# A two-layer graph network on one core: ten slots for streamed weights instead of six, and each weight piece in three or five transfers instead of two

## The reference

```python
h = relu(layernorm(x))
q, k, v = h @ wq.T + bq, h @ wk.T + bk, h @ wv.T + bv
q2, k2, v2 = q @ wiq.T + biq, k @ wik.T + bik, v @ wiv.T + biv     # 16 heads of 64
attn = softmax(q2 k2^T / 8 + mask(edges, edge_type_5))
x = x + (attn v2) @ wo.T + bo
h = relu(layernorm(x))
u = h @ root + bias
for r in range(8):
    u = u + mean_over_edges_of_type_r(h) @ weight[r]
z = concat([u, h]) @ w_gate + b_gate
x = x + tanh(u) * z + h * (1 - z)
```

## Time and profile before

| | us |
|---|---|
| median of 3 runs | 229.99 (228.32 to 234.5) |
| the profiled execution, its own time | 230.86 |
| span of its trace | 228.7 |
| TensorE (PE) matmuls busy | 217.3 |
| TensorE weight loads (PEld) busy | 210.8 |
| VectorE busy | 80.5 |
| GpSimd busy | 24.6 |
| ScalarE busy | 22.3 |

### The profile page before, as it was taken

One profiled execution on the slowest core, in us unless ns is written; L12 is line 12 of the kernel. 1 busy time (PEld: TensorE's weight loads), 2 busy tenths in 40 slices (PEclk: granted clock), 3 DMA queues, 4 the chain that ended last, 5 costly groups with the idle time before them and its releaser, 6 DMA issues.

```text
span 228.7 us, 10049 instructions
## 1 busy us (share of the span) xinstructions
PE 217.3 (95%) x4797; PEld 210.8 (92%) x4797; DVE 80.5 (35%) x138; ACT 22.3 (10%) x41; POOL 24.6 (11%) x53
## 2 busy tenths in 40 slices
PE   1999998999999999999999999999999999999894
PEld 1889998999999999799989999999999888999893
DVE  2459838051499731457466500000000000000614
ACT  2523000000020120313051000000000000000001
POOL 2255005400000000010003910000000000000000
PEclk9999999999999999999999999999999999999999
DMA  6999999999989989948981999999999999999202
GB/s 224 381 392 419 426 420 408 398 398 387 393 307 380 388 312 322 386 146 308 335 341 37 391 401 390 384 387 393 393 403 374 388 378 376 386 397 337 110 3 69
DMA packets 12363, 76.99 MB, mean 337 GB/s; under 512 B 2554, under 2 KB 2818, under 8 KB 3108
## 3 DMA queue, kind: packets, MB, share of 16 engines
q1 hardware_dynamic: 11792, 75.95, 85.9%
q10 hardware_dynamic: 532, 0.42, 0.6%
HBM read 75.97 MB, written 0.39 MB: 334 GB/s over the span
## 4 chain that ended last, share of the span: by engine, by line
PE 94%; DMA 2%; issue 1%; DVE 1%; ACT 0%
PE acc L779 81%; PE acc L1026 4%; DMA x_sb<-in_x 2%; PE turn L967 1%; PE side L827 1%; PE side L967 1%; PE side L1026 1%; PE turn L855 1%; DVE stats L504 1%; PE acc L797 1%; PE turn L797 0%; PE turn L871 0%; PE side L838 0%; PE turn L838 0%; PE acc L871 0%
## 5 line engine op out<-in xcount | busy, mean ns | idle before, releaser
L779 PE MATMUL acc<-mean,raw 128*64 128x96 f32 x2048 | 85.5, 246 | 1.4 <-issue 1.4
L779 PEld LDWEIGHTS acc<-mean,raw 128*64 128x64 f32 x2048 | 84.9, 137 | 1.8 <-issue 1.8
L779 PE MATMUL acc<-hT,raw 128*64 128x96 f32 x1024 | 44.7, 247 | 0.2
L779 PEld LDWEIGHTS acc<-hT,raw 128*64 128x64 f32 x1024 | 42.9, 137 | 1.5 <-issue 1.2
L742 DVE TENSOR_TENSOR uT<-acc,uT 128x384 f32<-128x384 f32 x2 | 1.1, 558 | 83.0 <-PE acc L779 83.0
L779 PE MATMUL acc<-qT,raw 128*64 128x96 f32 x512 | 22.0, 246 | 1.0 <-issue 1.0
L779 PEld LDWEIGHTS acc<-qT,raw 128*64 128x64 f32 x512 | 21.4, 137 | 1.3 <-issue 1.3
L779 PE MATMUL acc<-kT,raw 128*64 128x96 f32 x512 | 21.7, 246 | 0.0
L779 PEld LDWEIGHTS acc<-kT,raw 128*64 128x64 f32 x512 | 21.3, 137 | 0.3 <-issue 0.3
L779 PE MATMUL acc<-uT,raw 128*64 128x96 f32 x256 | 13.0, 271 | 0.0
L779 PEld LDWEIGHTS acc<-uT,raw 128*64 128x64 f32 x256 | 12.6, 156 | 0.3 <-ACT uT L408 0.2
(11 more groups left out here) (177 smaller groups left out, 149.7 us busy)
## 6 DMA issues: line engine op xcount, KB each, us to landing
raw<-in_weights SPq DMA_DIRECT2D x136, 512.0 KB, 5.6
raw<-in_weights SPq DMA_DIRECT2D x4, 1024.0 KB, 9.8
x_sb<-in_x SPq DMA_DIRECT2D x1, 192.0 KB, 3.7
x_sb<-in_x ACTq DMA_DIRECT2D x1, 192.0 KB, 3.8
out<-out_rows SPq DMA_DIRECT2D x1, 192.0 KB, 2.1
out<-out_rows ACTq DMA_DIRECT2D x1, 144.0 KB, 2.2
out<-out_rows SPq DMA_DIRECT2D x1, 48.0 KB, 2.5
bias_rows<-in_biases ACTq DMA_DIRECT2D x1, 36.0 KB
```

Source lines behind the costliest of these rows:

```text
L779: mm = pe.matmul(a[g * HD:(g + 1) * HD, b, c * N:(c + 1) * N], raw[:, s, at:at + HD], moving(k0 + k), start=opens and k0 == 0 and c == 0 a ...
```

## The change

`SLOTS` goes from 6 to 10, so `raw` takes 80 KB of each partition instead of 48 KB. `transfers(n)` returns a list of partition slices. Piece 0 remains one transfer. An odd piece goes in five: every second partition (64), a quarter (32), an eighth (16) and twice a sixteenth (8 and 8). An even piece goes in three of 64, 32 and 32. `landed` counts 16 per transfer as before. Nothing is changed on the other engines but the number of the slot and the value that each wait compares with.

```diff
-SLOTS = 6
+SLOTS = 10
...
 def transfers(n):
 
-    return 1 if n < 4 else 2
+
+
+    if n == 0:
+        return [slice(0, P)]
+    if n % 2:
+        return [slice(0, P, 2), slice(1, P, 4), slice(3, P, 8), slice(7, P, 16), slice(15, P, 16)]
+    return [slice(0, P, 2), slice(1, P, 4), slice(3, P, 4)]
...
-    return 16 * sum(transfers(i) for i in range(n % SLOTS, n + 1, SLOTS))
+    return 16 * sum(len(transfers(i)) for i in range(n % SLOTS, n + 1, SLOTS))
...
-                for j in range(transfers(n)):
-                    part = slice(j, P, transfers(n))
+                for part in transfers(n):
                     sp.dma_start(raw[part, n % SLOTS, :], weights[where, part]).then_inc(raw_landed[n % SLOTS], 16)
```

## The result

The changed kernel takes 262.09 us (median of 4 runs, 261.64 to 263.09), the kernel before 231.09 us in the same session (228.32 to 234.5). I had forecast 227.4 us and a range up to 232.5. The change costs 31 us, and nothing like that was in my sum.

What follows compares the result with a forecast made beforehand. TensorE was taken as the bound, losing 4.4 us to late instruction packets. All other terms counted 0, so 230.86 - 3.5 = 227.4 us, with a range of 225.8 to 232.5 us.

Steps and rivals of the forecast that it cites:

- What bounds the kernel: TensorE, busy 217.3 of 228.7 us, never waits for weights; late instruction packets, 128 matmuls apart, lose it 4.4 us.
- Ten slots, 0 by itself: SP can issue up to four pieces earlier, but nothing on TensorE's path waits for weights; worth 0.
- More issues on SP, 0 and at most 1 us at the start: Transfers rise from 140 to 286; a pair costs SP 4.5 us, hidden behind TensorE's 5.30.
- More small packets, 0: On each DMA engine, a pair ends in 8 small packets instead of 4: 0 to 0.35 us more, low end taken.
- The split of 8 partitions, 0: At worst eight DMA engines carry 17 rows per pair, falling back 2.5 us in all, within the 3 us lead.
- The instruction packets, a gain of 3.5 us: At TensorE's late instruction packets, smaller transfers shorten the wait; four fifths of the 4.4 us lost there is regained.
- The full queue: Rival: at TensorE's every 128th matmul, instruction packets wait behind ten slots' queue; 237 to 238 us, upper price 18.5 us; chance 0.17.
- The weight stream behind: Rival: loaded DMA engines need 5.72 us per pair, so TensorE waits 1 to 2 us; 228 to 231 us; chance 0.08.

Runs made afterwards that it cites:

- 64, 32, 16, 16: Changed kernel with the two 8-partition transfers of each odd piece replaced by one of 16; 262.93 us, ratio 1.137 to the kernel before.
- the three lines above: TensorE's waits for instructions in three ten-slot kernels: two transfers per piece (233.71 us), three (236.90 us), four of 32 on odd pieces (237.01 us).
- 64, 32, 32 and 32, 32, 32, 32: Changed kernel with every piece but the first in 64, 32, 32 (236.90 us), or with only odd pieces in four transfers of 32 (237.01 us).
- the kernel with halves: Kernel before with its two transfers as lower and upper 64 partitions instead of even and odd ones; 337.01 us, ratio 1.466.

## Why the prediction was wrong

*What bounds the kernel* was read rightly: TensorE, and what it loses at the late instruction packets, 128 matmuls apart. The changed kernel and every slow one of this study lose most time there, and only with the DMA under 240 GB/s do late weights add more than 3 us.

*Ten slots, 0 by itself*: 2.1% (0.3 to 3.9). The sentence that they keep more packets standing in the queues had the right effect in it, at a price of 0.

*More issues on SP, 0 and at most 1 us at the start*: an issue took 0.588 us at the median and not 0.539, with the gap behind it 0.63, so 8 x 0.63 = 5.0 us per pair against 5.30. Once the slots were full it stayed hidden. At the start it did not: SP's many issues and the slower DMA together made 1.7 us.

*More small packets, 0*: right, 419 GB/s with 52% more of them (762 against about 500). In the trace a small packet takes 9 ns at the median, far under my bound of 86.

*The split of 8 partitions, 0*: the unequal load was there, and it cost nothing beside 64, 32, 16, 16. But I asked only how many rows an engine gets. This is the step that failed: every term of the sum took the DMA's 418 GB/s of the earlier trace rows as given for any split, though these rows show only transfers of 64 and 128 partitions, spread over all 128. Transfers of 16 and 8 partitions were new, and the sum had no term for what they do to the rate. They took it to 341 GB/s from 20 to 60 us, and the two of 16 alone are worth about 26 us. Which property of them does it, the partitions that they cover or the single row for each engine, the runs leave open.

*The instruction packets, a gain of 3.5 us*: wrong in sign. The wait doesn't shrink with smaller transfers, as the three lines above show, nor with smaller rows. With rows of 8 KB it grows as the full queue drains more slowly: 5.4 to 10.5 us of waits at 406 to 420 GB/s, 21.8 at 382, 34.0 at 341, 59.2 at 289, over 70 at 222 to 234. (What there was to gain I had put at 4.4 us, from six pieces of the chain; the view of waits has 5.4 in twelve.)

*The rivals.* The full queue was the right one of the three in its place and its sign, with 237 to 238 us for 262, but not in its cause: the deeper queue by itself costs some 5 us, and the new transfers with six slots 25 to 27. Its price came from the loss of 0.3 us per packet in the stretch of the earlier trace rows; with the slower DMA it was 34.0/37 = 0.9 us. The range left it out. The weight stream behind was foretold at 5.72 us per pair; at 341 GB/s it is 2 x 1.049/0.341 = 6.15 us. By an estimate it would have bound the kernel at some 235 us even with every instruction in time (75.95 MB at some 330 GB/s, as in the page's full slices, is 230 us, and the start and the last piece come on top); no run shows that. The rule that I weighed against the change, the Trainium skill's of 1 MB or more in a transfer (DMA: Bandwidth & Descriptors, "Bandwidth"), was the wrong one for this case: 64, 32, 32 and 32, 32, 32, 32 hold 419 GB/s, as much as two of 64 with ten slots (420). The rule on ports stood in the Trainium skill too, and I had not weighed it.

## What to carry to other kernels

Before a load is cut into smaller transfers, look at which partitions each of them covers, not only at how many: cut a 128-partition tile by steps of 2 or 4, not into neighbouring blocks (47% slower here as two halves), and stop before a transfer is down to 16 partitions (8 to 32% slower here). A kernel that uses many small matmuls and a full DMA at once can pay for a slower DMA in late instructions before it pays in late data. An "issue" wait every 128 matmuls is the sign, and the ends of the packets in the instruction queue are the proof. A queue that is deeper than the lead needs gained nothing here (ten slots 2.1% slower than six, four 1.1% faster); try fewer slots as well as more.

## What I had not expected of the hardware

A few transfers of the wrong kind slow the others too: an eighth of the bytes in transfers of 16 partitions took the DMA from 419 to 342 GB/s and made 58% of all rows slower than 330 ns; half of the bytes in transfers to one side took it to 234, near the rate of a kernel that sends all of them that way (227). The source did not matter: neighbouring rows in HBM are read at 411 GB/s. With steps of 6 instead of 8 partitions almost nothing came back over the whole span, and why is open. And in the kernel with halves the lower clock cost next to nothing: with instructions as the limit, 128 matmuls and the wait behind them took 8.5 to 9.2 us with slow stretches and without.
